# Low parts of query and middle ahead of statistics and norms in VectorE's order, queries split straight from PSUM, and tile addresses at multiples of 512 bytes

## The chip, the cores and the metric

One core of one Trainium2 chip. The time is that of one execution on the device, in microseconds (us), as the median of several runs. The engines are TensorE (PE in the profile, its weight loads PEld), VectorE (DVE), ScalarE (ACT), GpSimd (POOL) and SyncE (SP, which issues most DMAs here).

## What is computed

The input is x, two sequences of 4096 tokens with 512 channels each, so 8192 tokens. The output is the sum of three things: x, an attention branch and a feed-forward branch, both on the normalised x.

```python
xn = layernorm(x)
# attention branch: linear attention, 32 heads of 16 channels
q, k, v = split(relu(xn @ qkv_weight.T))            # each 8192 x 512
vk = einsum('bnhe,bnhd->bhed', [v, 1], k)           # per sequence and head
att = vk_q[..., :16] / (vk_q[..., 16:] + 1e-15)     # vk_q = vk applied to q
y1 = att @ proj_weight.T + proj_bias
# feed-forward branch
cont = sigmoid(xn @ enc_w + enc_b) @ s2c_w + s2c_b  # 512 -> 1024 -> 64
...                                                 # router: the best 2 of 8 experts for each token
moe = sum of w_e * (relu(cont @ e_w1 + e_b1) @ e_w2 + e_b2)   # 64 -> 512 -> 64
rates = sigmoid(moe @ c2s_w + c2s_b)                # 64 -> 1024
y2 = layernorm(sigmoid(rates @ dec_w + dec_b)) * ln_g + ln_b  # 1024 -> 512
out = x + y1 + y2
```

## The kernel before

**Split matmuls.** Every large product is made from float32 values that are split in two: a high part (written as fp32r by ScalarE) and a low part (the value less its high part, by VectorE). `pass3` (L102 to L105) multiplies high weights by the high input, low weights by the high input, and high weights by the low input: three matmuls of 128x128 stationary and 128x512 moving values for each pair of chunks.

**Four stages**, each a block of five engine programs that are written out by hand and tied by semaphores. A block of tokens has 512 tokens (NB = 16), a tile 128 (TT = 64). `front` (A) normalises, transposes and encodes: for each block 8 groups of 12 encoder matmuls (stationary `enc`, moving `xs`), each followed by a pair on `s2c`, with transposes after some. `keyvalue` (B) makes key and value for each tile: 2 x 12 matmuls (L946 to L948; stationary `xs`, moving `wk` or `wv`), then 8 outer products of 258 columns on `kh`, `kl` and `v`. `experts` (C) runs 39 groups of 512 gathered tokens with 4 x 4 matmuls each on `wt`, and two times four transposes between them; SyncE loads each group's expert weights `wt` and tokens `gt`, and stores the result `yo` three groups later; `yo` has three buffers, so VectorE's `close_tile` (L1246) waits for an older store. While this goes on the weights of the last stage are loaded and split. `decode` (D) makes query, attention output, decoder and the sum.

**The decode stage.** TensorE's order for block i, with the second half of block i-1 worked in: for each of four chunks m of the query `query(i, m)` (12 matmuls of `pass3` into the bank bX[m % 2]; stationary `wq`, moving `xsd`); after chunk 0 `middle(i)` (four transposes of the mixture `mo` of both experts' outputs), after chunks 1 and 2 `rates(i, m - 1)` (the content product, L1460 and L1461, on `midh` and `midl`); and `denominators(i, m - 1)` (L1468, L1469, on `qh` and `ql`). Then `attend(i - 1, t)` for four tiles (the output product, L1486 to L1488, 12 matmuls on `qnh`, `qnl` and `mh`, `ml`), four decoder biases, and 8 x 12 decoder matmuls (L1509 to L1511) with six more content products and four `fan` products between them. The banks bX serve the query and the output product in turn, so `attend(i - 1, 0)` waits for the plain query of chunk 2, and `attend(i - 1, 1)` for that of chunk 3.

ScalarE's `query(i, m)` first writes the plain query `q` (relu of the bank, L1370) and then from it the high part `qh` (L1373); then `middle(i)` writes `midh` (L1378), and `rates` takes a tanh (L1384) and its high part (L1392). VectorE's side of the same things is `query` (`ql` from `q` and `qh`, L1572), `middle` (`midl` from the bank and `midh`, L1577) and `rates` (`ratel`, L1582). For block i-1 VectorE also has per tile `stats` (batch statistics of `out`, L1587, and after the fourth the aggregates L1592), `norm` (L1597), `add` (L1605, with the root `rs` that GpSimd makes of the variances, L1334) and `attend` (adds the output product, L1612). GpSimd adds the bias to the next x in four operations (L1354), from the first output addition on. In block 0 there is nothing behind, and TensorE puts `decoder_sum` (16 matmuls, L1494 and L1495) after the query; VectorE works on its result (L1627).

**Addresses.** `Memory.put` places each tile in the first gap that is free in its stages, at a multiple of 32 bytes. The first free byte is 16,512. From the order and the sizes in `place` the starts follow; modulo 512 bytes they are: 224 for `enc`, `xs0`, `xs1`, `s2c` and `wk_h`; 384 for `wk_l`, `wv`, `sph`, `spl`, `kh`, `kl`, `v`, `dec`, `wq`, `c2s`, `fan`, `rc2`, `rows`, `pick_bias`, `mh`, `ml`, `den`, `qh`, `ql`, `qnh`, `qnl`, `rateh` and `ratel`; 0 for `ch`, `cl`, `hidh`, `hidl`, `xsd`, `midh` and `midl`; 128 for `ident`; and 384, 416, 448 and 480 for `wt0` to `wt3`. The chunks inside a tile that matmuls address start at multiples of 512 bytes from the tile's start, except in `v` (rows of 258 values) and in the last part of `wt` (at value 1026).

Of the kernel before, what the change touches and what calls it, by code (L numbers as in the profile page):

```python
# [5 lines left out]
ALU = mybir.AluOpType  # L6
# [6 lines left out]
P = 128  # L13
# [17 lines left out]
DEN_EPS = 1e-15  # L31
VW = 2 * P + 2


NS = 2 * TOK // BLK + NE - 1

E1A, E2, B2, E1B = 0, EH, 2 * EH, 2 * EH + 2
EW = 3 * EH + 2

# [32 lines left out]
class Memory(dict):  # L72


    def __init__(self, nc):
        super().__init__()
        self.nc, self.placed, self.floor = nc, [], (nc.sbuf_base + 31) // 32 * 32

    def put(self, stages, name, shape, dt=F32):
        size = 4  # L80
        for n in shape[1:]:
            size *= n
        size = (size + 31) // 32 * 32
        taken = sorted((a, b) for a, b, s in self.placed if set(s) & set(stages))
        at = self.floor
        for a, b in taken:
            if at + size <= a:
                break
            at = max(at, b)
        assert at + size <= self.nc.sbuf_usable_end, (name, at + size)  # L90
        self.placed.append((at, at + size, stages))
        self[name] = self.nc.alloc_sbuf_tensor_at(name, list(shape), dt, offset=at)
        return at
# [14 lines left out]
def place(nc):  # L108
# [69 lines left out]
    for n in ("kh", "kl"):  # L178
        put("B", n, [P, 2, DIM], F32R)
    put("B", "v", [P, 2, KC, VW], F32R)  # L180
    put("BC", "total", [P, KC, VW])
# [38 lines left out]
    put("Cc", "eo", [P, 2, BLK])  # L220
    put("Cc", "c2s_raw", [P, HID])
    put("Cc", "fanf", [P, KC, P])
    put("Cc", "blank", [P, BLK])
    put("Cc", "pbf", [P, P])
    put("Cc", "onesf", [MOE, BLK])
    put("Cc", "bias2", [P, 2, DIM])
# [610 lines left out]
def keyvalue(nc, d, T, S):  # L837
    with ExitStack() as ctx:
# [95 lines left out]
        def _(pe):  # L934
# [17 lines left out]
            def outer(n):  # L952
# [6 lines left out]
                for g in range(KC):  # L959
                    s = slice(g * P, (g + 1) * P)  # L960
                    pe.matmul(bA[g][:, 0:VW], kh[:, n % 2, s], v[:, n % 2, g, :], start=(n % HALF == 0), stop=False)
                    m = pe.matmul(bA[g][:, 0:VW], kl[:, n % 2, s], v[:, n % 2, g, :], start=False,
                                  stop=(n % HALF == HALF - 1))
# [75 lines left out]
def experts(nc, d, T, S):  # L1039
    with ExitStack() as ctx:  # L1040
# [12 lines left out]
        def _(sp):  # L1053
# [6 lines left out]
            def load_expert(g):  # L1060
                if g >= 4:
# [3 lines left out]
                rows = P if g < 4 else BIAS_ROWS  # L1065
                sp.dma_start(f32(wt[g % 4][:, 0:E1B]), d["ew"][bass.ds(e, 1), :, 0:E1B].rearrange("e p w -> (e p) w"))\
                    .then_inc(S[f"wt_in{g % 4}"], 16)
# [10 lines left out]
            for g in range(NS):  # L1078
# [3 lines left out]
                if g == 2:  # L1082
                    sp.dma_start(T["c2s_raw"][:, :], d["c2s_w"][:, :]).then_inc(S["w_in3"], 16)
                    sp.dma_start(T["dec_raw"][:, :, :], d["dec_w"][:, :].rearrange("p (c n) -> p c n", n=DIM))\
# [5 lines left out]
                if g == 8:  # L1090
                    sp.wait_ge(S["den_out"], BATCH)
                    sp.wait_ge(S["m_done"], BATCH * KC)
                    sp.dma_start(f32(T["xsd"][:, :, :, :]), d["xs"][0]).then_inc(S["xsd_in"], 16)
                if g >= 6:
# [7 lines left out]
        def _(pool):  # L1102
            fanf, pbf = T["fanf"], T["pbf"]
            pool.memset(T["onesf"][:, :], 1.0).then_inc(S["c_consts"], 1)
            pool.wait_ge(S["c_consts"], 1)
# [123 lines left out]
        def _(dve):  # L1229
# [3 lines left out]
            for i in range(2):  # L1233
                dve.tensor_copy(cl[MOE:P, i, :], T["onesf"][:, :]).then_inc(S["cl_ones"], 1)

# [51 lines left out]
def decode(nc, d, T, S, out_dram):  # L1287
    with ExitStack() as ctx:
# [76 lines left out]
        def _(act):  # L1365
            def query(i, m):
                n = i * KC + m
                act.wait_ge(S["q_done"], n + 1)
                wait(act, S["qnl_out"], n - KC + 1)
                act.activation(q[:, m, :], bX[m % 2][:, :], ACT.Relu).then_inc(S["q_out"], 1)  # L1370
                act.wait_ge(S["q_out"], n + 1)
                wait(act, S["den_done"], n - 1)
                act.activation(qh[:, m % 2, :], q[:, m, :], ACT.Copy).then_inc(S["qh_out"], 1)  # L1373

# [25 lines left out]
            for i in range(NB):  # L1400
                for m in range(KC):
                    query(i, m)
                    if m == 0 and i:
                        middle(i)
                    if 1 <= m <= 2 and i:
                        rates(i, m - 1)
                if i == 0:
# [143 lines left out]
        def _(dve):  # L1551
# [16 lines left out]
            def query(i, m):  # L1568
                n = i * KC + m
                dve.wait_ge(S["qh_out"], n + 1)  # L1570
                wait(dve, S["den_done"], n - 1)
                dve.tensor_tensor(ql[:, m % 2, :], q[:, m, :], f32(qh[:, m % 2, :]), ALU.subtract).then_inc(S["ql_out"], 1)  # L1572

# [68 lines left out]
            for i in range(NB + 1):  # L1642
                ahead, behind = i < NB, i > 0
                if behind:
                    for t in range(NT):
                        stats(i - 1, t)
                    norm(i - 1, 0)
                if ahead and behind:
                    query(i, 0)
                    middle(i)  # L1650
                if behind:
                    add(i - 1, 0)
                    norm(i - 1, 1)
                    add(i - 1, 1)
                if ahead and behind:
                    query(i, 1)
                    rates(i, 0)
                if behind:
                    norm(i - 1, 2)
                    norm(i - 1, 3)  # L1660
# [110 lines left out]
```

## Time and profile before

| | us |
|---|---|
| median of 3 runs | 2007.07 (2006.65 to 2007.4) |
| the profiled execution | 2008.04 |
| its span in the trace | 2006.3 |
| stage A, TensorE from and to | 12.7 to 501.5 |
| stage B | 501.5 to 933.2 |
| stage C | 933.2 to 1135.3 |
| stage D | 1135.3 to 2002.7 |

The span is the time between the first and the last instruction that the profile holds; the profiled execution's own time has 1.7 us more around it. Shares of busy time over the span are TensorE 97%, VectorE 53%, ScalarE 41%, GpSimd 19%. The granted clock of TensorE is 0.989 of full over the execution, and full in nearly all slices.

How to read the rows: a row of the timeline is its start, its duration, the engine, the line of the kernel, the operation, output and inputs by name, shapes and number; in brackets stands how long the engine had been idle before it and what ended that. Matmuls are pipelined, so that they overlap in the listing: their pace is the distance of starts.

### The profile page before, as it was taken

What the parts mean: (1) busy time and instruction counts of PE and PEld (TensorE: products, weight loads), DVE (VectorE), ACT (ScalarE), POOL (GpSimd) and SP (SyncE); (2) the same over time, 40 slices, a digit from 0 to 9 for tenths busy, and PEclk for the clock granted to TensorE, in tenths of its full rate; (3) what the DMA queues carried; (4) which work ended last, traced back from release to release, by engine and by line L of the source; (5) the groups of instructions that cost most, each with busy time, mean ns of one, the idle gap of its engine ahead of it and who ended that gap; (6) DMA issues with size and microseconds to landing.
All of it is one profiled execution on the core that took longest, in us unless ns stands there. A gap on an engine that the chain in (4) does not pass through costs nothing. (4 is left out here: it accounts for less than half of the span.)

```text
span 2006.3 us, 24926 instructions
## 1 busy us (share of the span) xinstructions
PE 1944.9 (97%) x8980; PEld 1587.0 (79%) x8980; DVE 1055.2 (53%) x1863; ACT 812.9 (41%) x1359; POOL 390.4 (19%) x428
## 2 busy tenths in 40 slices
PE   7999999998999999998999889999999999999998
PEld 5888888887888888886788668888888888888886
DVE  6555555553442222223888555555555566566654
ACT  4545454544112221113777443443434444344442
POOL 1000000000004444421000212223222222222320
PEclk9999999999999999998999989999999999999999
DMA  5562333342123332223877502222222222221210
GB/s 204 229 226 79 127 150 123 138 153 74 63 88 113 116 113 107 97 82 143 280 231 236 171 24 90 90 90 90 90 89 89 89 88 89 83 69 72 80 69 32
DMA packets 74825, 233.93 MB, mean 117 GB/s; under 512 B 9856, under 2 KB 15952, under 8 KB 68176
## 3 DMA queue, kind: packets, MB, share of 16 engines
q1 hardware_dynamic: 66432, 219.58, 30.7%
q0 software_dynamic: 8272, 12.76, 2.1%
q8 instruction: 72, 1.18, 0.2%
q14 instruction: 49, 0.40, 0.1%
HBM read 151.95 MB, written 80.36 MB: 116 GB/s over the span
## 5 line engine op out<-in xcount | busy, mean ns | idle before, releaser
L103 PE MATMUL A_E<-xs,enc_h 128*128 128x512 f32 x512 | 207.6, 405 | 0.0
L1582 DVE TENSOR_TENSOR ratel<-rate,rateh 128x512 fp32r<-128x512 f32 x128 | 88.4, 691 | 217.4 <-ACT rateh L1392 217.4
L105 PE MATMUL A_E<-xs,enc_h 128*128 128x512 f32 x512 | 202.4, 395 | 0.0
L104 PE MATMUL A_E<-xs,enc_l 128*128 128x512 f32 x512 | 201.7, 394 | 0.0
L1509 PE MATMUL D_D<-dec_h,rateh 128*128 128x512 f32 x512 | 200.0, 391 | 0.0
L1510 PE MATMUL D_D<-dec_l,rateh 128*128 128x512 f32 x512 | 199.9, 390 | 0.0
L1511 PE MATMUL D_D<-dec_h,ratel 128*128 128x512 f32 x512 | 199.4, 389 | 0.0
L1384 ACT ACTIVATE rate<-D_Y,cols 128x512 f32<-128x512 f32 x128 | 87.7, 685 | 264.5 <-PE D_Y L1461 261.6
L571 DVE TENSOR_TENSOR spl<-sp_t,sph 128x512 fp32r<-128x512 f32 x128 | 88.6, 692 | 196.5 <-ACT sph L393 196.5
L871 POOL DMA_INDIRECT slots_scratch<-ctok,idx x128 | 123.5, 964 | 250.6 <-DVE v L999 123.5
L389 ACT ACTIVATE sp_t<-A_E,cols 128x512 f32<-128x512 f32 x128 | 88.1, 688 | 200.3 <-PE A_E L105 198.3
L1341 POOL DMA_INDIRECT ga<-eo_scratch,idx x64 | 66.3, 1036 | 371.6 <-DVE ratel L1582 192.6
L999 DVE SCALAR_TENSOR_TENSOR v<-B_KV,v 128x512 fp32r<-128x512 f32 x64 | 44.3, 692 | 175.0 <-ACT v L900 174.9
L900 ACT ACTIVATE v<-B_KV 128x512 fp32r<-128x512 f32 x64 | 38.4, 600 | 205.2 <-PE B_KV L948 205.2
L1354 POOL TENSOR_TENSOR xd<-xd,bias 128x512 f32<-128x512 f32 x64 | 80.4, 1281 | 178.6 <-DVE out L1612 178.6
L103 PEld LDWEIGHTS A_E<-xs,enc_h 128*128 128x128 f32 x512 | 96.9, 189 | 22.4 <-DVE xs L559 3.2
L105 PEld LDWEIGHTS A_E<-xs,enc_h 128*128 128x128 f32 x512 | 96.5, 189 | 21.9
L104 PEld LDWEIGHTS A_E<-xs,enc_l 128*128 128x128 f32 x512 | 96.9, 189 | 19.6
L1510 PEld LDWEIGHTS D_D<-dec_l,rateh 128*128 128x128 f32 x512 | 96.2, 188 | 20.5
L1511 PEld LDWEIGHTS D_D<-dec_h,ratel 128*128 128x128 f32 x512 | 96.1, 188 | 20.6
L1509 PEld LDWEIGHTS D_D<-dec_h,rateh 128*128 128x128 f32 x512 | 96.2, 188 | 20.5
L993 DVE SCALAR_TENSOR_TENSOR kl<-B_KV,kh 128x512 fp32r<-128x512 f32 x64 | 44.2, 691 | 129.1 <-ACT kh L896 129.1
(283 smaller groups left out, 4748.9 us busy)
## 6 DMA issues: line engine op xcount, KB each, us to landing
xs_scratch<-xs SPq DMA_DIRECT2D x16, 2048.0 KB, 8.5
xsd<-xs_scratch SPq DMA_DIRECT2D x16, 2048.0 KB, 7.9
xs<-xs_scratch SPq DMA_DIRECT2D x14, 2048.0 KB, 8.7
wt<-ew_scratch SPq DMA_DIRECT2D x39, 513.0 KB, 3.8
x<-in_x SPq DMA_DIRECT2D x16, 1024.0 KB, 5.4
xd<-in_x SPq DMA_DIRECT2D x16, 1024.0 KB, 5.2
out_y<-out SPq DMA_DIRECT2D x64, 256.0 KB, 2.0
slots_scratch<-zt SPq DMA_DIRECT2D x1, 9984.0 KB
```

The source lines that it names most:

```text
L103: pe.matmul(out, w_hi, x_hi, start=start, stop=False)
L104: pe.matmul(out, w_lo, x_hi, start=False, stop=False)
L105: return pe.matmul(out, w_hi, x_lo, start=False, stop=stop)
L389: act.activation(T["sp_t"][:, m % 2, :], bE[m % 2][:, :], ACT.Tanh, bias=T["enc_b"][:, m:m + 1], scale=0.5).then_inc(S["sp_out"], 1)
L571: dve.tensor_tensor(T["spl"][:, n % 3, :], T["sp_t"][:, m % 2, :], f32(T["sph"][:, n % 3, :]), ALU.subtract)\
L871: pool.indirect_dma_start(d["slots"][:, :], bass.IndirectOffsetOnAxis(ap=T["idx2" if second else "idx1"][:, t:t + 1], axis=0), T["ctok"][: ...
L1354: pool.tensor_tensor(x[i % 2][:, t, :], x[i % 2][:, t, :], T["bias"][:, :], ALU.add)\
L1384: act.activation(rate[:, k % 2, :], bY[:, :], ACT.Tanh, bias=T["c2s_b"][:, k:k + 1], scale=0.5)\
L1509: pe.matmul(bD[t][:, :], rateh[:, n % 3, o], T["dec_h"][:, k, :], start=False, stop=False)
L1510: pe.matmul(bD[t][:, :], rateh[:, n % 3, o], T["dec_l"][:, k, :], start=False, stop=False)
L1511: m = pe.matmul(bD[t][:, :], ratel[:, n % 3, o], T["dec_h"][:, k, :], start=False, stop=(k == HC - 1))
L1582: dve.tensor_tensor(ratel[:, n % 3, :], rate[:, k % 2, :], f32(rateh[:, n % 3, :]), ALU.subtract)\
```

## The change

1. VectorE's order in `decode`: the low parts of query chunk 0 and of the middle come ahead of the fourth statistic, the aggregates and the first norm; the first two adds come after the low parts of chunk 1 and of the first rates.
2. ScalarE's and VectorE's `query`: the high part is now the relu of the bank itself and is written first, and the low part is taken by VectorE from the bank (the larger of it and 0, less the high part). The plain query is written by ScalarE from the bank after the low part, behind `middle` or `rates`.
3. `Memory.put` starts every tile of 512 bytes or more at a multiple of 512. Rows of `v` are 384 values long (258 used), and the last part of `wt` starts at value 1152. After this every tile that a large matmul reads, and every chunk in it, starts at a multiple of 512 bytes. To make room, `onesf` is dropped (the first rows of `eo` carry the ones), and `c2s_raw` shares memory with a tile of stage B.
4. For that reason the load of `c2s_raw` moves from group 2 of stage C to group 8, ahead of the load of `xsd` and the store of `yo` in SyncE's queue. It is used in group 16.

```diff
-E1A, E2, B2, E1B = 0, EH, 2 * EH, 2 * EH + 2
-EW = 3 * EH + 2
+E1A, E2, B2, E1B = 0, EH, 2 * EH, 2 * EH + P
+EW = 3 * EH + P
...
+        step = 512 if size >= 512 else 32
         size = (size + 31) // 32 * 32
-        at = self.floor
+        at = (self.floor + step - 1) // step * step
         for a, b in taken:
             if at + size <= a:
                 break
-            at = max(at, b)
+            at = max(at, (b + step - 1) // step * step)
...
-    put("B", "v", [P, 2, KC, VW], F32R)
+    put("B", "v", [P, 2, KC, VROW], F32R)
...
                 if g == 2:
-                    sp.dma_start(T["c2s_raw"][:, :], d["c2s_w"][:, :]).then_inc(S["w_in3"], 16)
                     sp.dma_start(T["dec_raw"][:, :, :], d["dec_w"][:, :].rearrange("p (c n) -> p c n", n=DIM))\
...
                 if g == 8:
                     sp.wait_ge(S["den_out"], BATCH)
                     sp.wait_ge(S["m_done"], BATCH * KC)
+                    sp.dma_start(T["c2s_raw"][:, :], d["c2s_w"][:, :]).then_inc(S["w_in3"], 16)
                     sp.dma_start(f32(T["xsd"][:, :, :, :]), d["xs"][0]).then_inc(S["xsd_in"], 16)
...
             def query(i, m):
                 n = i * KC + m
                 act.wait_ge(S["q_done"], n + 1)
+                wait(act, S["den_done"], n - 1)
+                act.activation(qh[:, m % 2, :], bX[m % 2][:, :], ACT.Relu).then_inc(S["qh_out"], 1)
+                if m == 0 and i:
+                    middle(i)
+                if 1 <= m <= 2 and i:
+                    rates(i, m - 1)
+                act.wait_ge(S["ql_out"], n + 1)
                 wait(act, S["qnl_out"], n - KC + 1)
                 act.activation(q[:, m, :], bX[m % 2][:, :], ACT.Relu).then_inc(S["q_out"], 1)
-                act.wait_ge(S["q_out"], n + 1)
-                wait(act, S["den_done"], n - 1)
-                act.activation(qh[:, m % 2, :], q[:, m, :], ACT.Copy).then_inc(S["qh_out"], 1)
...
                 dve.wait_ge(S["qh_out"], n + 1)
                 wait(dve, S["den_done"], n - 1)
-                dve.tensor_tensor(ql[:, m % 2, :], q[:, m, :], f32(qh[:, m % 2, :]), ALU.subtract).then_inc(S["ql_out"], 1)
+                dve.scalar_tensor_tensor(out=ql[:, m % 2, :], in0=bX[m % 2][:, :], scalar=0.0,
+                                         in1=f32(qh[:, m % 2, :]), op0=ALU.max, op1=ALU.subtract)\
+                    .then_inc(S["ql_out"], 1)
...
                 if behind:
-                    for t in range(NT):
+                    for t in range(NT - 1):
                         stats(i - 1, t)
-                    norm(i - 1, 0)
                 if ahead and behind:
                     query(i, 0)
                     middle(i)
                 if behind:
-                    add(i - 1, 0)
+                    stats(i - 1, NT - 1)
+                    norm(i - 1, 0)
                     norm(i - 1, 1)
-                    add(i - 1, 1)
                 if ahead and behind:
                     query(i, 1)
                     rates(i, 0)
                 if behind:
+                    add(i - 1, 0)
+                    add(i - 1, 1)
                     norm(i - 1, 2)
                     norm(i - 1, 3)
```

## Rows read from the trace of the kernel before

**Rows 1.** The page: busy time of each engine, share of the span, instructions.

```profile
PE 1944.9 (97%) x8980; PEld 1587.0 (79%) x8980; DVE 1055.2 (53%) x1863; ACT 812.9 (41%) x1359; POOL 390.4 (19%) x428
```

**Rows 2.** Waits of PE: who waited for whom, us, times, longest.

```profile
PE D_Y L1460 <- DVE midl L1577: 9.7, 16, 1.4
```

**Rows 3.** Timeline of all engines, one decode block.

```profile
1513.09 2.47 DVE L1587 BATCH_NORM_STATS2 st<-out 128x6 f32<-128x512 f32 x4
...
1514.30 0.60 ACT L1370 ACTIVATE q<-D_X 128x512 f32<-128x512 f32 x1 [1.60 <-PE D_X L105]
...
1515.46 0.58 ACT L1378 ACTIVATE midh<-D_Y 128x512 fp32r<-128x512 f32 x1
...
1516.01 0.79 DVE L1597 SCALAR_TENSOR_TENSOR out<-out,mv,ln_g 128x512 f32<-128x512 f32 x1
...
1517.10 0.40 PE L105 MATMUL D_X<-xsd,wq_h 128*128 128x512 f32 x1
...
1518.06 0.50 PE L1460 MATMUL D_Y<-midh,c2s 128*128 128x512 f32 x1 [0.56 <-DVE midl L1577]
...
1518.39 0.39 PE L1461 MATMUL D_Y<-midl,c2s 128*128 128x512 f32 x1
```

**Rows 4.** Timeline of PE: starts in runs of stage A, B and D.

```profile
203.62 0.40 PE L104 MATMUL A_E<-xs,enc_l 128*128 128x512 f32 x1
...
205.48 0.39 PE L103 MATMUL A_E<-xs,enc_h 128*128 128x512 f32 x1
...
206.16 0.40 PE L476 MATMUL A_S<-sph,s2c 128*128 128x512 f32 x1
...
600.07 0.40 PE L946 MATMUL B_KV<-wv_h,xs 128*128 128x512 f32 x1
...
605.41 0.40 PE L948 MATMUL B_KV<-wk_h,xs 128*128 128x512 f32 x1
...
1511.31 0.40 PE L103 MATMUL D_X<-xsd,wq_h 128*128 128x512 f32 x1
...
1513.87 0.39 PE L105 MATMUL D_X<-xsd,wq_h 128*128 128x512 f32 x1
...
1529.22 0.39 PE L1486 MATMUL D_X<-mh,qnh 128*128 128x512 f32 x1
...
1537.16 0.39 PE L1488 MATMUL D_X<-mh,qnl 128*128 128x512 f32 x1
```

**Rows 5.** Timeline of the end: the first add of the last block.

```profile
1990.28 0.75 DVE L1605 SCALAR_TENSOR_TENSOR out<-out,rs,xd 128x512 f32<-128x512 f32 x1 [0.96 <-POOL rs L1334]
```

**Rows 6.** Timeline of decode block 0.

```profile
1145.75 4.99 POOL L1354 TENSOR_TENSOR xd<-xd,bias 128x512 f32<-128x512 f32 x4
...
1147.30 4.61 DVE L1572 TENSOR_TENSOR ql<-q,qh 128x512 fp32r<-128x512 f32 x2 [2.57 <-ACT qh L1373]
...
1148.82 0.40 PE L105 MATMUL D_X<-xsd,wq_h 128*128 128x512 f32 x1
...
1151.36 0.50 PE L1468 MATMUL D_Y<-qh,den 128*128 128x512 f32 x1 [2.14 <-DVE ql L1572]
...
1153.07 0.63 PE L1494 MATMUL D_D<-dec_h,ones 128*128 128x512 f32 x1
...
1156.94 0.39 PE L1495 MATMUL D_D<-dec_l,ones 128*128 128x512 f32 x1
```

**Rows 7.** Timeline of a steady decode block: GpSimd's bias additions.

```profile
1529.74 5.03 POOL L1354 TENSOR_TENSOR xd<-xd,bias 128x512 f32<-128x512 f32 x4 [12.04 <-DVE out L1612]
...
1532.14 0.69 DVE L1612 TENSOR_TENSOR out<-D_X,out 128x512 f32<-128x512 f32 x1 [1.42 <-PE D_X L1488]
```

**Rows 8.** Timeline of stage C and list of DMA issues (KB, us to landing).

```profile
973.75 0.37 SPq L1093 DMA_DIRECT2D xsd<-xs_scratch  x1
...
984.10 0.69 DVE L1246 TENSOR_REDUCE yo<-C_Y 128x256 f32<-128x512 f32 x1 [3.42 <-DMA eo_scratch<-yo]
...
c2s_raw<-in_c2s_w SPq DMA_DIRECT2D x1, 512.0 KB, 3.6
```

More of the change, by code:

```diff
@@ L32 @@
 VW = 2 * P + 2
+VROW = 3 * P
 NS = 2 * TOK // BLK + NE - 1
-E1A, E2, B2, E1B = 0, EH, 2 * EH, 2 * EH + 2
-EW = 3 * EH + 2
+E1A, E2, B2, E1B = 0, EH, 2 * EH, 2 * EH + P
+EW = 3 * EH + P
 BIAS_ROWS = 80
@@ L220, in place @@
     put("Cc", "eo", [P, 2, BLK])
-    put("Cc", "c2s_raw", [P, HID])
+    put("c", "c2s_raw", [P, HID])
     put("Cc", "fanf", [P, KC, P])
@@ L224, in place @@
     put("Cc", "pbf", [P, P])
-    put("Cc", "onesf", [MOE, BLK])
     put("Cc", "bias2", [P, 2, DIM])
@@ L960, in outer @@
                     s = slice(g * P, (g + 1) * P)
-                    pe.matmul(bA[g][:, 0:VW], kh[:, n % 2, s], v[:, n % 2, g, :], start=(n % HALF == 0), stop=False)
-                    m = pe.matmul(bA[g][:, 0:VW], kl[:, n % 2, s], v[:, n % 2, g, :], start=False,
+                    pe.matmul(bA[g][:, 0:VW], kh[:, n % 2, s], v[:, n % 2, g, 0:VW], start=(n % HALF == 0), stop=False)
+                    m = pe.matmul(bA[g][:, 0:VW], kl[:, n % 2, s], v[:, n % 2, g, 0:VW], start=False,
                                   stop=(n % HALF == HALF - 1))
@@ L1065, in load_expert @@
                 rows = P if g < 4 else BIAS_ROWS
-                sp.dma_start(f32(wt[g % 4][:, 0:E1B]), d["ew"][bass.ds(e, 1), :, 0:E1B].rearrange("e p w -> (e p) w"))\
+                sp.dma_start(f32(wt[g % 4][:, 0:B2 + 2]), d["ew"][bass.ds(e, 1), :, 0:B2 + 2].rearrange("e p w -> (e p) w"))\
                     .then_inc(S[f"wt_in{g % 4}"], 16)
@@ L1103, in _ @@
             fanf, pbf = T["fanf"], T["pbf"]
-            pool.memset(T["onesf"][:, :], 1.0).then_inc(S["c_consts"], 1)
+            pool.memset(T["eo"][0:MOE, 0, :], 1.0).then_inc(S["c_consts"], 1)
             pool.wait_ge(S["c_consts"], 1)
@@ L1233, in _ @@
             for i in range(2):
-                dve.tensor_copy(cl[MOE:P, i, :], T["onesf"][:, :]).then_inc(S["cl_ones"], 1)
+                dve.tensor_copy(cl[MOE:P, i, :], T["eo"][0:MOE, 0, :]).then_inc(S["cl_ones"], 1)
             def content(g):
@@ L1402, in _ @@
                     query(i, m)
[L1403 to L1406, printed above, removed]
                 if i == 0:
```

## Prediction

> **What bounds the kernel now.** I read the page first: it says which engine is full. TensorE is busy for 97% of the span [rows 1], so time can go in two ways only: TensorE waits less, or its own instructions follow each other more closely. The list of waits comes next. Its largest entry inside the steady loop is the content product's wait for `midl`, 16 times [rows 2]. To see what that costs, the timeline of one decode block is read in order [rows 3]; to see how closely matmuls follow each other, I take the starts of long runs without a wait and divide by the intervals [rows 4]. The listed durations (0.39 or 0.40 us) overlap and don't show it; the starts do.
>
> Order in the block [rows 3]: the last matmul of the second query chunk starts at 1517.10, the next could start 0.23 later, at 1517.33. It starts at 1518.06, and its successor only 0.33 after it. So 0.73 + 0.10 = 0.83 us are lost. What is late is `midl`. Its inputs are there early: `midh` starts at 1515.46 (0.58 long). VectorE meanwhile does four statistics, the aggregates and a norm up to 1516.80, and only then `ql` and `midl`.
>
> **Part 1: VectorE's and ScalarE's order.** In the new order three statistics (4 take 2.47, so 3 take 1.86) end at 1514.95. ScalarE writes `qh` as its first action on the product, so from 1514.30 for about 0.60, to 1514.90; `midh` follows to 1515.5. VectorE: `ql` 1514.95 to 1515.65, `midl` to 1516.35. TensorE wants it at 1517.33: one us to spare. The stall goes: 15 blocks x 0.83 = 12.4 us (the sixteenth wait is block 0's, where all is serial).
>
> Who is late next? I drop the 1500 of the times. Behind `midl` (16.35) come the fourth statistic and the aggregates (about 1.1 together, by the pace of the same rows), two norms (1.5) and `ql` of chunk 1, written by about 19.7; its high part is ready at 18.1. TensorE wants it after the content product, the first denominators, twelve query matmuls and the next content product: 17.33 + 18 x 0.23 = 21.5. Then come the low rates, two adds and two norms (3.7) and `ql` 2, by 24.0, wanted at 24.7. ScalarE now holds the plain query back until `ql` is written, and behind it in its queue stand the next chunk's high part and rates. Plain chunk 2 is there at 24.7, and TensorE's output product needs its bank at 25.2; plain chunk 3 at 27.5, wanted at 28.4. The tanh of the rates stands ahead of the new wait and isn't delayed. POOL's root is ready 0.96 after a norm of 0.79 [rows 3, 5], 1.75 behind the aggregates, so at 19.2; the adds now stand at 20.3. The thinnest place has 0.5 us. I take no new stall; with that cover gone, each 0.1 us of lateness costs 15 x 0.1 = 1.5 us. The bounds of this part are 0 and 12.4.
>
> In the last block a norm now fills the wait of 0.96 us for POOL's root [rows 5]: 0.7 us, on the chain that ends the kernel.
>
> **Part 2: the low part straight from PSUM.** One instruction for one instruction, both 128x512. In steady blocks nothing changes. In block 0 it does [rows 6]: POOL adds the bias from 1145.75 to 1150.74, and two `ql` instructions of VectorE take 4.61, where others of this size take 0.69 each [rows 7]. TensorE's denominators start at 1151.36 where they could have started at 1149.05, and the decoder's sum behind them runs partly with durations of 0.63 in place of 0.39 (the granted clock's 1.2 GHz level). The last of its 16 matmuls starts at 1156.94; without stall and at full clock it is 1149.05 + 17 x 0.227 = 1152.91. Difference 4.0 us. VectorE's first work after it waits for that sum, so all of it is passed on. Would the new instruction be held up as well? It reads one tile in PSUM and one in SBUF, as the output addition does, and that one takes 0.69 in the middle of POOL's four additions [rows 7]. So 4.0 us; bounds 0 and 4.0.
> The Trainium skill (SBUF — State Buffer, section "SBUF: two separate sides") states a lock between VectorE with two SBUF inputs and a GpSimd operation that reads SBUF; the trace agrees (4.61 against 0.69), and the sum is the same by it.
>
> **Part 3: addresses.** Offsets are those of the section on the kernel, in bytes modulo 512. Four kinds of run without waits [rows 4]:
> - output product, stationary 384, moving 384: (1537.16 - 1529.22) / 35 = 226.9 ns
> - query, stationary 384, moving 0: (1513.87 - 1511.31) / 11 = 232.7 ns
> - key and value, stationary 224, moving 224 or 384: (605.41 - 600.07) / 23 = 232.2 ns
> - encoder, 224 and 224, behind transposes: the first 8 intervals 232.5 ns, the next 3 (206.16 - 205.48) / 3 = 226.7 ns.
>
> The encoder and the query run the same three lines in the same pattern, and only one of them settles at 227. So neither the pattern nor a multiple of 64 bytes decides (224 isn't one). What fits all four is whether the two operands have the same offset: then the pace settles at 227 after some 8 matmuls, otherwise it stays near 232.5. After the change all matmul operands are at 0. The sum:
> - query: 768 matmuls x 5.8 ns = 4.5 us
> - key and value: 1536 x 5.3 = 8.1, less 64 settlings after the outer products, each 8 x 5.6 = 45 ns, 2.9: 5.2 us
> - encoder: half of 128 groups of twelve follow only the `s2c` pair (224 on 384), which I take as what unsettles them: 64 x 45 ns = 2.9, and the pairs themselves, 256 x 3 ns = 0.8: 3.7 us
> - experts: 624 matmuls, but transposes come every 4 or 12: at most 3.6, I take 1
> - decoder: 96 content pairs (384 on 0) between fast matmuls, about 0.02 us each (half a settling): 1.9 us
>
> Together 16 us. It could be nothing (0), or up to 22 if nothing has to settle any more.
> The opposing rule in the Trainium skill is on the same page and in the same section: within the engine side only the port pair that VectorE and GpSimd share causes contention, and TensorE waits on nobody. By it addresses do nothing for matmuls, and that is the first rival. The two paces of one code [rows 4] speak against it.
>
> **Part 4: the moved load.** `c2s_raw`, 512 KB, now stands in SP's queue before the 2048 KB of `xsd` and the store of `yo` behind that. In the trace that store is what VectorE waits for at 984.10, 3.42 us, and TensorE behind VectorE [rows 8]. `xsd` and the store behind it take from 973.75 to 984.0, so some 4.9 us for each MB: 512 KB more is 2.5 us, all of it on the path, at the slow 1.2 GHz level perhaps a little more. Bounds: 0 (if the transfers overlap better) and 3.6, its own time to landing [rows 8]. I take 2.5. At its old place its absence lets the weights behind it land earlier, at nothing to 0.5. Memory set from another tile, the 1536-byte row of `v`, 512 bytes of padding in `wt`: the same instructions and bytes, nothing.
>
> **Sum.** 12.4 + 0.7 + 4.0 + 16 - 2.5 = 30.6. The profiled execution took 2008.04; 2008.04 - 30.6 = 1977.4. The median is 1.0 lower than the profiled execution: 1976.
>
> **Rivals.**
> 1. Addresses do nothing. For it: no row varies the address alone. Against: the same code at two paces. 2007.1 - 14.6 = 1992.
> 2. The plain query is held too long. ScalarE's queue waits for `ql`, and the output product or the denominators stall in place of the content product. For it: ScalarE's new wait, with 0.5 us of slack at its thinnest. Against: that slack. It gives the 12.4 us back: 1988. The point is a `ql` of chunk 2 more than 0.5 us later than worked out.
> 3. Offset 0 is itself the slow one, not the difference. For it: `xsd`, `ch`, `cl` and `midh` are all moving operands at 0, and all their runs are slow. Against: key and value are slow without a 0. Then nothing gains and the fast runs join the slow: some 150 matmuls a block x 16 plus half of the encoder's 1536, 3170 x 5.8 ns = 18.4 us. 2007.1 - 14.6 + 18.4 = 2011, slower. It decides from a pace of about 231.5 ns in the output product on.
> 4. More than forecast: everything settles, and the outer products (258 columns) tighten as well: 1966.
>
> **Numbers.** Forecast 0.62, rival 1 0.20, rival 2 0.07, rival 3 0.07, rival 4 0.04. The forecast's own range is 1968 to 1984: parts 3 and 4 between half and full. The range for 8 in 10 must reach rival 1, the largest other case: 1967 to 1994. A difference of 0.2% (4 us) is about what can be told from no change. Faster 0.92 (all but rival 3 and a bad mix), within 0.2% 0.04, slower 0.04.
>
> **What would show it.** Order: the wait for `midl` is left in block 0 only, and the content product starts 0.23 after the query; a block is shorter by 0.83 + (4.5 + 1.9) / 16 = 1.2 us. PSUM: no `ql` over 0.75 us, none of TensorE's waits on `ql`, and the sum in block 0 without matmuls of 0.63. Addresses: starts in the query 227 apart and in key and value after some 8 matmuls. Load: the wait for the `yo` store near 6 us. Wrong it would be if query starts stay 232.7 apart, or a wait of the output product or the denominators shows up 15 times.

## The result and the profile after

| | before | after |
|---|---|---|
| median, us (4 runs each) | 2007.24 (2006.65 to 2007.52) | 1971.43 (1969.36 to 1973.64) |
| the profiled execution | 2008.04 | 1971.89 |
| its span | 2006.3 | 1970.1 |
| stage A, TensorE from its start to its end | 488.8 | 483.2 (12.5 to 495.7) |
| stage B | 431.7 | 421.8 (to 917.5) |
| stage C | 202.1 | 203.5 (to 1121.0) |
| stage D | 867.4 | 845.5 (to 1966.5) |

The ratio is 0.9822 [0.9805, 0.9839] (in brackets the 95% interval, here and below): the kernel is faster by 35.8 us. Forecast were 1976 (31 us) and a range of 1967 to 1994. The table says at once where to look: 21.9 us come from the decode stage, 9.9 and 5.6 from B and A, in which nothing but addresses was changed, and stage C lost 1.4.

The page, busy time of each engine. TensorE is as full as before [rows 1], and its busy time is 26.4 us less for the same number of instructions:

```profile
PE 1918.5 (97%) x8980; PEld 1586.5 (81%) x8980; DVE 1049.0 (53%) x1863; ACT 809.9 (41%) x1359; POOL 390.8 (20%) x428
```

The waits of PE (us in total, times, longest), from the second of the list on:

```profile
PE C_O L1212 <- DVE hidl L1261: 6.1, 4, 3.6
PE D_X L1488 <- DVE out L1616: 3.9, 1, 3.9
PE D_Y L1453 <- DVE mo L1565: 3.8, 1, 3.8
...
PE D_Y L1462 <- DVE midl L1581: 1.4, 1, 1.4
```

The wait for `midl`, 9.7 us in 16 times [rows 2], is left once, in block 0. Nothing has taken its place: no wait of the output product, the denominators or the content product that comes 15 times. The first line is the largest wait of the experts' products; it was 5.2 us before.

Timeline of one decode block, VectorE, ScalarE and TensorE in order:

```profile
1488.93 1.87 DVE L1591 BATCH_NORM_STATS2 st<-out 128x6 f32<-128x512 f32 x3
...
1490.07 0.60 ACT L1372 ACTIVATE qh<-D_X 128x512 fp32r<-128x512 f32 x1 [1.54 <-PE D_X L108]
1490.56 0.59 ACT L1384 ACTIVATE midh<-D_Y 128x512 fp32r<-128x512 f32 x1
1490.71 0.67 DVE L1574 SCALAR_TENSOR_TENSOR ql<-D_X,qh 128x512 fp32r<-128x512 f32 x1
1491.31 0.68 DVE L1581 TENSOR_TENSOR midl<-D_Y,midh 128x512 fp32r<-128x512 f32 x1
...
1492.85 0.39 PE L108 MATMUL D_X<-xsd,wq_h 128*128 128x512 f32 x1
1493.08 0.39 PE L1462 MATMUL D_Y<-midh,c2s 128*128 128x512 f32 x1
...
1498.41 0.68 DVE L1574 SCALAR_TENSOR_TENSOR ql<-D_X,qh 128x512 fp32r<-128x512 f32 x1
...
1499.12 0.60 ACT L1379 ACTIVATE q<-D_X 128x512 f32<-128x512 f32 x1 [0.38 <-DVE ql L1574]
...
1500.78 0.39 PE L1488 MATMUL D_X<-mh,qnh 128*128 128x512 f32 x1
```

Read against [rows 3]: `midl` ends at 1491.99, and the content product starts at 1493.08, 0.23 behind the last matmul of the query. It had 1.09 us to spare (forecast: one us). The thinnest place of the new order is the plain query of chunk 2: ScalarE ends it at 1499.72, the output product needs its bank at 1500.78, so 1.06 us are left where 0.5 was forecast.

Timeline of block 0:

```profile
1131.39 5.04 POOL L1356 TENSOR_TENSOR xd<-xd,bias 128x512 f32<-128x512 f32 x4
...
1133.50 0.69 DVE L1574 SCALAR_TENSOR_TENSOR ql<-D_X,qh 128x512 fp32r<-128x512 f32 x1 [2.79 <-ACT qh L1372]
...
1135.30 0.39 PE L108 MATMUL D_X<-xsd,wq_h 128*128 128x512 f32 x1
...
1139.45 0.40 PE L1497 MATMUL D_D<-dec_l,ones 128*128 128x512 f32 x1
```

In the middle of GpSimd's additions `ql` takes 0.69, where two took 4.61 [rows 6]. From the query's last matmul to the decoder sum's last it is 4.15 us, and it was 1156.94 - 1148.82 = 8.12.

Timeline of PE: starts in runs of stage A (behind transposes, and behind the pair on `s2c`), B (right behind the outer products, and the next half) and D:

```profile
201.19 0.39 PE L107 MATMUL A_E<-xs,enc_l 128*128 128x512 f32 x1
...
203.48 0.39 PE L108 MATMUL A_E<-xs,enc_h 128*128 128x512 f32 x1
...
204.16 0.39 PE L106 MATMUL A_E<-xs,enc_h 128*128 128x512 f32 x1
...
205.97 0.39 PE L108 MATMUL A_E<-xs,enc_h 128*128 128x512 f32 x1
...
584.64 0.40 PE L948 MATMUL B_KV<-wv_h,xs 128*128 128x512 f32 x1
...
587.16 0.39 PE L950 MATMUL B_KV<-wv_h,xs 128*128 128x512 f32 x1
587.39 0.39 PE L948 MATMUL B_KV<-wk_h,xs 128*128 128x512 f32 x1
...
589.88 0.39 PE L950 MATMUL B_KV<-wk_h,xs 128*128 128x512 f32 x1
...
1493.98 0.39 PE L106 MATMUL D_X<-xsd,wq_h 128*128 128x512 f32 x1
...
1496.48 0.39 PE L108 MATMUL D_X<-xsd,wq_h 128*128 128x512 f32 x1
```

The query goes at (1496.48 - 1493.98) / 11 = 227.3 ns, where it went at 232.7 [rows 4]. Key and value: (587.16 - 584.64) / 11 = 229.1 ns behind the outer products, then (589.88 - 587.39) / 11 = 226.4. The encoder: (203.48 - 201.19) / 10 = 229.0 behind transposes, and (205.97 - 204.16) / 8 = 226.3 right behind the pair on `s2c`, which no longer unsettles anything.

A run of matmuls settles, as I call it, when its starts come to stand some 226.6 ns apart. To add this up I took every distance from the start of a 512-column matmul to the start of the next matmul, if it is under 260 ns, in each stage, less 226.6 ns each, and call the sum the excess:

| excess over 226.6 ns a matmul, us | A | B | C | D | sum |
|---|---|---|---|---|---|
| before | 7.8 | 9.8 | 3.1 | 8.2 | 28.9 |
| after | 2.5 | 1.8 | 2.2 | 1.65 | 8.2 |
| gain | 5.3 | 8.0 | 0.9 | 6.6 | 20.7 |

With only those distances counted in which the next matmul has 512 columns too, the gain is 20.2 us.

Timeline of stage C, the queue of SyncE and what follows:

```profile
958.28 0.37 SPq L1094 DMA_DIRECT2D c2s_raw<-in_c2s_w  x1
958.69 0.43 SPq L1095 DMA_DIRECT2D xsd<-xs_scratch  x1
959.17 0.43 SPq L1076 DMA_DIRECT2D eo_scratch<-yo  x1
...
969.45 0.69 DVE L1248 TENSOR_REDUCE yo<-C_Y 128x256 f32<-128x512 f32 x1 [4.27 <-DMA eo_scratch<-yo]
...
970.79 0.80 PE L1212 MATMUL C_O<-hidh,wt 128*128 128x512 f32 x1 [3.61 <-DVE hidl L1261]
971.38 0.63 PE L1213 MATMUL C_O<-hidl,wt 128*128 128x512 f32 x1
```

VectorE's wait for the store is 4.27 us, 0.85 more than before [rows 8]. Behind it TensorE waits 3.61 us (before 2.73), and then 11 of its 512-column matmuls run at the 1.2 GHz level (durations of 0.63; the granted clock is 0.50 of full from 973.3 to 976.4); before there were 5. Such a matmul starts some 0.43 us behind its predecessor in place of 0.23, so six more are 1.2 us.

### The profile page after: what moved, and what is told of

It is laid out like the page before. It is cut to its first block and busy times, and to the rows that moved or that the text cites. A ratio compares the mean times of both kernels' runs of the same rounds, so it can differ in the third digit from the quotient of the medians.

```text
span 1970.1 us, 24926 instructions
## 1 busy us (share of the span) xinstructions
PE 1918.5 (97%) x8980; PEld 1586.5 (81%) x8980; DVE 1049.0 (53%) x1863; ACT 809.9 (41%) x1359; POOL 390.8 (20%) x428
## 5 line engine op out<-in xcount | busy, mean ns | idle before, releaser
L1512 PEld LDWEIGHTS D_D<-dec_l,rateh 128*128 128x128 f32 x512 | 96.4, 188 | 20.2
```

The source lines that it names most:

```text
L1512: pe.matmul(bD[t][:, :], rateh[:, n % 3, o], T["dec_l"][:, k, :], start=False, stop=False)
```

## The experiments

Each kernel is compared with the kernel before on the same chip; the medians of before there are 2005.93 (e1, e2, e3, e5), 2005.63 (e4, e6, e7) and 2006.36 (e8, e9). "Before" and "after" in the edits are the two kernels of this study.

**e1: the addresses alone.** Everything of the change but the decode stage's code, which is that of before.

Two of the lines of after that it takes back:

```diff
-                for t in range(NT - 1):
+                for t in range(NT):
                     stats(i - 1, t)
...
-                act.activation(qh[:, m % 2, :], bX[m % 2][:, :], ACT.Relu)
+                act.activation(q[:, m, :], bX[m % 2][:, :], ACT.Relu)
```

> The kernel after with the decode stage's code of before: addresses, the row of v, the padding of wt and the moved load stay; the new order and the low part from PSUM are undone. Theory of the prediction, with the sizes that the trace after shows (stage A 5.6 us shorter, B 9.9 shorter, C 1.4 longer, and in D matmuls after matmuls some 6.6 us closer): 2007.2 - 20.7 = 1986.5. The wait for midl (15 x 0.56 to 0.74) and the long ql of block 0 are back. Rival (the addresses do little and the order gave most of the 36 us): 1995 or more, with query starts still near 232 apart.

Measured: 1988.17 (1986.07 to 1990.25), ratio 0.9913 [0.9897, 0.993], 17.8 us less than before. The excess is 2.6, 1.8, 2.2 and 2.1 us in A to D, as after. The waits of PE:

```profile
PE D_Y L1462 <- DVE midl L1579: 11.3, 16, 1.4
PE C_O L1212 <- DVE hidl L1261: 6.3, 5, 3.6
...
PE D_Y L1470 <- DVE ql L1574: 2.4, 1, 2.4
```

What follows: half of the gain is made by tile addresses, with no matmul of the loops that got faster added, dropped or reordered. (The moved load, which costs time, is in e1 as well.) The first line holds something that I had not worked out: the wait for `midl` is 11.3 us, 1.6 more than before, since a query that ends earlier only leads to a longer wait. Addresses alone therefore lose 1.6 us that the new order gives back.

**e2: order and PSUM alone.** The kernel before with the decode code of after.

Two of the places (memory, `v`, `wt` and the load of `c2s_raw` are those of before):

```diff
-                act.activation(q[:, m, :], bX[m % 2][:, :], ACT.Relu)
+                act.activation(qh[:, m % 2, :], bX[m % 2][:, :], ACT.Relu)
...
-                for t in range(NT):
+                for t in range(NT - 1):
                     stats(i - 1, t)
```

> The kernel before with the decode stage's code of after: new order and low part from PSUM, addresses and loads as before. Theory: 12.4 + 4.0 + 0.7 us, 2007.2 - 17.1 = 1990; starts of key, value and query stay at 232 to 233 apart, the wait for midl is gone in 15 blocks. Rival (addresses alone): 2003 or more. If the two parts add up, e1 and e2 together give 1986.5 + 1990 - 2007.2 = 1969.3, against 1971.4 measured for the whole.

Measured: 1988.65 (1988.14 to 1989.15), ratio 0.9913 [0.9897, 0.993], 17.3 us less. The excess is that of before (7.7, 9.8, 3.2 and 7.95 us), and the wait for `midl` is left in block 0 alone (1.4 us, once). The two halves together, 0.87% and 0.87%, make 1.74%; the whole change made 1.78%. They add up within the error.

**e5: VectorE's order alone.** As e2, but `ql` is still taken from the plain query in SBUF, and the plain query is still written first.

```diff
-                    for t in range(NT):
+                    for t in range(NT - 1):
                         stats(i - 1, t)
-                    norm(i - 1, 0)
                 if ahead and behind:
                     query(i, 0)
                     middle(i)
                 if behind:
-                    add(i - 1, 0)
+                    stats(i - 1, NT - 1)
+                    norm(i - 1, 0)
                     norm(i - 1, 1)
-                    add(i - 1, 1)
                 if ahead and behind:
                     query(i, 1)
                     rates(i, 0)
                 if behind:
+                    add(i - 1, 0)
+                    add(i - 1, 1)
```

> The kernel before with VectorE's new order alone: ScalarE writes the plain query first and VectorE takes ql from two SBUF tiles, as before. Theory: qh is 0.6 us later than in the whole change, midl still ends at about 1517.0 of the old clock against 1517.33 wanted, so the stall of 0.83 goes in 15 blocks and 0.7 us at the end: 2007.2 - 13.1 = 1994. Block 0 keeps its ql of 4 us and TensorE's wait of 2.1 behind it. So e5 less e2 is the price of the PSUM part: 4.0 us. Rival (the split from PSUM is what makes room for midl): the wait for midl stays, smaller, and the time is 1999 or more.

Measured: 1991.04 (1990.86 to 1991.26), ratio 0.9926 [0.9909, 0.9942], 14.9 us less. So point 2 of the change (the low part from PSUM, together with ScalarE's new order) is worth 1991.04 - 1988.65 = 2.4 us, not 4.0. It lies in block 0 (the table below: 6.59 - 4.17 = 2.42): from the first to the last of the 16 `midl` both kernels take as long, 762.5 and 762.4 us. In the steady blocks VectorE's order alone removes the stall. One line's view in e5 and in e2 (duration in ns, least, median, most), each in its own fence:

```profile
L1572 DVE TENSOR_TENSOR ql<-q,qh x64: 676/692/4035, 1140.3 to 1932.6; 128x512 fp32r<-128x512 f32 x64
```

```profile
L1572 DVE SCALAR_TENSOR_TENSOR ql<-D_X,qh x64: 676/691/693, 1138.5 to 1929.3; 128x512 fp32r<-128x512 f32 x64
```

One of 64 takes 4.0 us when both inputs are in SBUF, and none does when one is in PSUM; the median is the same. The two lines agree with the lock that the Trainium skill describes (SBUF — State Buffer, "SBUF: two separate sides"), between VectorE with two SBUF inputs and a GpSimd operation that reads SBUF: 4.035 against 0.693 us at most. The operation changed with the source, so that the lines alone don't separate the two.

Why 2.4 and not 4.0 can be read from the same stretch as above, the query's last matmul to the decoder sum's last, in every kernel:

| | ql from | us |
|---|---|---|
| before | SBUF | 8.12 |
| e5 | SBUF | 6.59 |
| e1 | SBUF | 6.80 |
| e9 (below) | SBUF | 6.81 |
| e2 | PSUM | 4.17 |
| after | PSUM | 4.15 |

With the stall at full clock it is 2.4 to 2.7 us more than without. Only in the profiled execution of before did 8 matmuls behind it run at the 1.2 GHz level (the granted clock is 0.69 of full from 1151.4 to 1156.9), another 1.3 to 1.5 us; e1, e5 and e9 have the same stall (2.2 to 2.4 us) and none there. Whether most executions of before have these 8, the one profile of it can't say.

**e3: all at 224 instead of 0.** After, with every tile of 512 bytes or more at 224 modulo 512.

```diff
+PHASE = 224
...
-        at = (self.floor + step - 1) // step * step
+        def up(b):
+            return (b - PHASE + step - 1) // step * step + PHASE
+        at = up(self.floor)
```

> The kernel after with every tile of 512 bytes or more at 224 modulo 512 in place of 0: no operand is at a multiple of 64 bytes, all differences are 0. Theory (the difference between the two operands decides): the same as after, 1971, starts 227 apart in key, value and query. Rival (multiples of 512, or of 64, decide by themselves): starts near 232, 7300 matmuls x 5.5 ns = 40 us at most, 1990 to 2011.

Measured: 1972.21 (1971.27 to 1972.8), ratio 0.9832 [0.9815, 0.9848]. Key and value, the half behind the values' half, timeline of PE:

```profile
588.93 0.39 PE L953 MATMUL B_KV<-wk_h,xs 128*128 128x512 f32 x1
...
591.42 0.39 PE L955 MATMUL B_KV<-wk_h,xs 128*128 128x512 f32 x1
```

(591.42 - 588.93) / 11 = 226.4 ns, as after. No large tile is at a multiple of 512, or even of 64, and all is as fast. What decides is how the two operands stand to each other. Rival 3, offset 0 as the slow one, was refuted by the result itself, where every operand is at 0 and the runs are fast.

**e4: single differences.** After, with some tiles moved so that a product's operands differ: `xsd` by 256, `qnh` and `qnl` by 128, `rateh` and `ratel` by 64, `xs` by 32.

```diff
+PHASE = {'xsd': 256, 'qnh': 128, 'qnl': 128, 'rateh': 64, 'ratel': 64, 'xs0': 32, 'xs1': 32}
...
+        phase = PHASE.get(name, 0) if step == 512 else 0
```

> The kernel after with tiles of one product moved against each other, a different distance in each stage: xsd at 256 modulo 512 (wq at 0), qnh and qnl at 128 (mh and ml at 0), rateh and ratel at 64 (dec at 0), xs0 and xs1 at 32 (enc, wk and wv at 0). It asks how fine the rule is. If any difference modulo 512 unsettles a run, all four settle nowhere: the output product and the decoder go to 232 (2300 matmuls x 5.5 ns = 13 us), the query to 232.7 (4.5), encoder, key and value back to their old pace (15): about 2003. If only a difference in the low bits counts (a multiple of 64 is as good as 0), then the query, the output product and the decoder stay at 227 and stage A and B alone are slow: 1986. The rival that no rule of addresses holds (the pace came from something else in the change): 1971.

Measured: 2004.45 (2002.02 to 2005.94), ratio 0.9996 [0.9986, 1.0007]. The whole gain is gone, though the new order is in: the decoder, the encoder and the output product, which were fast or half fast before, are now slow as well. All but one product behave as expected. Timeline of PE, a query chunk and then two tiles of the output product:

```profile
1514.32 0.39 PE L111 MATMUL D_X<-xsd,wq_h 128*128 128x512 f32 x1
...
1516.81 0.39 PE L113 MATMUL D_X<-xsd,wq_h 128*128 128x512 f32 x1
...
1524.38 0.40 PE L1493 MATMUL D_X<-mh,qnh 128*128 128x512 f32 x1
...
1529.75 0.39 PE L1495 MATMUL D_X<-mh,qnl 128*128 128x512 f32 x1
```

The output product (128 apart) goes at (1529.75 - 1524.38) / 23 = 233.5 ns. The query, 256 apart, goes at (1516.81 - 1514.32) / 11 = 226.4: as fast as with no difference at all. "The same offset modulo 512" was too narrow.

**e8: is the period 256?** After, with 256 between the operands of the encoder, of key and value and of the decoder, and 128 in the query (`xsd` 128) and in the output product (`qnh`, `qnl` 384).

```diff
+PHASE = {'xs0': 256, 'xs1': 256, 'rateh': 256, 'ratel': 256, 'qnh': 384, 'qnl': 384, 'xsd': 128}
```

> The kernel after with other distances between the two operands: xs0 and xs1 at 256 modulo 512 (encoder, key and value), rateh and ratel at 256 (decoder), qnh and qnl at 384 (output product), xsd at 128 (query); enc, wk, wv, dec, mh, ml and wq stay at 0. e4_differences found 256 as good as 0 in the query and 128, 64 and 32 bad. Theory (what counts is the difference modulo 256): encoder, key, value and decoder stay at 227, the output product (384, which is 128 modulo 256) goes to 232 to 233 and the query (128) too: 768 x 6 ns each = 9 us, 1980. Rival (256 was good in the query for a reason of the query's own): the decoder's 1536 and stage A and B slow as well, 2003.

Measured: 1980.61 (1979.87 to 1982.31), ratio 0.9871 [0.9856, 0.9887]. Key and value, and the output product:

```profile
595.45 0.39 PE L953 MATMUL B_KV<-wk_h,xs 128*128 128x512 f32 x1
...
597.94 0.39 PE L955 MATMUL B_KV<-wk_h,xs 128*128 128x512 f32 x1
...
1506.89 0.39 PE L1493 MATMUL D_X<-mh,qnh 128*128 128x512 f32 x1
...
1515.03 0.40 PE L1495 MATMUL D_X<-mh,qnl 128*128 128x512 f32 x1
```

226.4 ns with 256 between the operands, (1515.03 - 1506.89) / 35 = 232.6 with 384. The rule passed a test that was made for it. All kernels together, mean distance of starts (those under 260 ns) over all matmuls of a product:

| difference of starts modulo 256 | product and kernel | ns |
|---|---|---|
| 0 | output product, before / after | 227.2 / 226.7 |
| 0 | query, after / e3 | 227.5 / 227.5 |
| 0 (256) | query e4; decoder e8 | 228.2; 227.1 |
| 0 (256) | key halves of key and value, e8 | 226.7 |
| 32 | key and value, e4; encoder, e4 | 233.2; 232.7 |
| 64 | decoder, e4 | 233.2 |
| 128 | query, before / e8 | 232.6 / 232.5 |
| 128 | output product, e4 / e8 | 233.2 / 232.6 |
| 160 | value, before | 233.9 |
| 0 for `wk_h`, 160 for `wk_l` | key, before | 232.1 |

The last row says that the rule holds for a run as a whole: two of three key matmuls had equal offsets before, and with every third at 160 the run didn't settle.

**e9: the smallest edit.** The kernel before, with `xsd` at 384 modulo 512, where `wq` is.

```diff
             at = max(at, b)
+        if name == "xsd":
+            at = (at - 384 + 511) // 512 * 512 + 384
```

> The kernel before with one tile moved: xsd starts at 384 modulo 512 in place of 0, like wq (the tiles behind it move on by 384 bytes); all code and all other offsets of matmul operands as before. Theory: the query's 768 matmuls settle at 227: 4.5 us less than before, 0.2%, and all other paces unchanged. Rival (a single tile says nothing, the pace hangs on the whole layout or on the order): no change in the query's starts.

Measured: 2001.4 (1998.78 to 2002.93), ratio 0.9976 [0.9966, 0.9987], 5.0 us less. Timeline of PE, one query chunk:

```profile
1504.39 0.39 PE L106 MATMUL D_X<-xsd,wq_h 128*128 128x512 f32 x1
...
1506.88 0.39 PE L108 MATMUL D_X<-xsd,wq_h 128*128 128x512 f32 x1
```

226.4 ns. The excess of D falls from 8.2 to 2.15, and in A, B and C it stays (8.0, 9.9, 3.2). The 6.1 us in D are more than the query's: the first free gap behind the moved `xsd` puts `midh` and `midl` at 384 too, where `c2s` is, so that the content pairs settle as well. And they are more than the 5.0 measured, for the reason of e1: the wait for `midl` grows from 9.7 to 11.3. 6.1 - 1.6 = 4.5.

**e6: the moved load, three groups earlier.** After, with `c2s_raw` loaded at group 5 instead of 8.

```diff
+                if g == 5:
+                    sp.wait_ge(S["den_out"], BATCH)
+                    sp.wait_ge(S["m_done"], BATCH * KC)
+                    sp.dma_start(T["c2s_raw"][:, :], d["c2s_w"][:, :]).then_inc(S["w_in3"], 16)
                 if g == 8:
-                    sp.dma_start(T["c2s_raw"][:, :], d["c2s_w"][:, :]).then_inc(S["w_in3"], 16)
```

> The kernel after with the load of c2s_raw at group 5 of stage C in place of group 8 (with the same two waits for the memory, moved with it), so that no other large load stands ahead of xsd and the store. Theory: VectorE's wait for the yo store falls from about 4.3 to about 3.4 or less, and TensorE's matmuls at the low clock behind it from 11 to 6: 1 to 2.5 us less than after, 1969 to 1970.5. Rival (the extra wait in the trace after has another cause): the wait stays as long, 1971.4.

Measured: 1970.41 (1968.0 to 1971.03), ratio 0.9819 [0.9803, 0.9836]. In the trace the wait for the store of `yo` is 3.6 us (before 3.4, after 4.3), TensorE's for `hidl` 5.6 in all, and 6 matmuls behind it are slow instead of 11; in time the difference from after can't be told from none. So the cost of the moved load is read from the traces alone.

**e7: `xsd` in parts.** As e6, and `xsd` is loaded in eight parts of 256 KB, one every third group, each behind a store of `yo`.

```diff
                 if g == 8:
-                    sp.dma_start(f32(T["xsd"][:, :, :, :]), d["xs"][0]).then_inc(S["xsd_in"], 16)
...
                     store(g - 6)
+                if g >= 9 and g % 3 == 0 and g < 33:
+                    h, c = divmod((g - 9) // 3, KC)
+                    sp.dma_start(f32(T["xsd"][:, h, c, :]), d["xs"][0][:, h, c, :]).then_inc(S["xsd_in"], 16)
...
-                    pe.wait_ge(S["xsd_in"], 16 * i + 16)
+                    pe.wait_ge(S["xsd_in"], 16 * i + 16 * 2 * KC)
```

> The kernel of e6_c2s_early with the 2048 KB of xsd loaded in 8 parts of 256 KB, one behind the store of every third group from group 9 on. Theory: no store waits behind a long transfer, VectorE's wait for the yo store and the low clock behind it are gone: 3.8 + 2.2 us less than after, 1965.5. Rival (the queues are nearly full in this stage, and the delay only spreads): several waits for stores or weights of 1 us each, and 1969 or more.

Measured: 1966.35 (1965.02 to 1967.78), ratio 0.9801 [0.9785, 0.9817]: 4.1 us under e6, with no overlap of the two kernels' runs, and the fastest kernel of this study. The groups by line, and the waits of PE:

```profile
L1250 DVE TENSOR_REDUCE yo<-C_Y 128x256 f32<-128x512 f32 x39 | 26.3, 674 | 1.7 <-PE C_Y L1188 1.7
```

```profile
PE C_O L1214 <- DVE hidl L1263: 2.7, 4, 1.1
```

VectorE waits for no store at all; the slowest of the 39 landed 5.6 us after its issue, where it was 10.0 in e6. TensorE's wait for `hidl` is 2.7 us where e6 has 5.6, and the stretch of slow matmuls in the middle of stage C isn't there: 2.9 + 6 x 0.2 = 4.1 us. Stage C takes 197.4 us, 3.7 less than in e6 and 6.1 less than after. The cost that the moved load added to was there before the change, and it goes when the 2 MB transfer no longer stands ahead of a store in one piece. e7 changed both the size of the parts and their place in the queue; which of the two does it isn't shown.

## Why the prediction held, and where its sizes were off

Against the profiled executions the sum was 30.6 us, and 2008.04 - 1971.89 = 36.15 came. The terms, with what the traces give for each:

| term | forecast | by the traces |
|---|---|---|
| order in steady blocks | 12.4 | 12.4 |
| last block | 0.7 | 0.8 |
| `ql` from PSUM, block 0 | 4.0 | 4.0 in these two executions, 2.4 by e5 and e2 |
| addresses | 16 | 20.7 |
| moved load | -2.5 | -0.9, and -1.2 for slow matmuls behind it |
| extents of the 1.2 GHz level elsewhere | 0 | +0.6 |

They sum to 36.4 (the outer products' 0.5, below, isn't among them). The last row counts the 512-column matmuls at the low level that the rows above it don't hold, 61 before and 58 after, at 0.2 us each.

**Order: right, in mechanism and size.** Forecast was a block shorter by 1.2 us. The 16 `midl` stand from 1162.9 to 1938.9 before and from 1145.4 to 1902.9 after: (776.0 - 757.5) / 15 = 1.23 us; without the first distance, which holds the end of block 0, the median block went from 52.72 to 51.45, so 1.27. The stall itself can be read in e5, which has before's addresses: from the last query matmul of chunk 1 to the second content matmul it is 1.289 us in mean before and 0.466 in e5, and 15 x 0.823 = 12.3. Rival 2, the plain query held too long, didn't happen: the wait that it needs is in no list, and the thinnest place has 1.06 us. e5 measured order and last block at 14.9, 1.7 more than the 13.2 of the two rows. If most executions of before have the 8 matmuls at the low level that e5 has not, they explain 1.3 to 1.5 of it; but the runs of before also range over 4.5 us, so that this stays open. In the last block TensorE's wait for `out` fell from 4.7 to 3.9.

**PSUM: right, but priced with something that isn't the stall's alone.** The step is "without stall and at full clock it is 1149.05 + 17 x 0.227 = 1152.91. Difference 4.0 us". The stall itself was 2.14 [rows 6]; most of the rest were matmuls at the low level, which three other executions with the same stall had not. The term is 2.4 by e5 and e2, which differ in point 2 of the change alone, and 4.0 only against an execution that has them.

**Addresses: right rule, too small a term, and too narrow a rule.** The step that failed in size is "Together 16 us"; 20.7 came, inside its bounds of 0 to 22. Rival 1 (nothing) is refuted by e1, e4 and e9, rival 3 by the result and by e3. The part on each product:
- key and value: 5.2 forecast, 8.0 by the excess. I took the slow pace from one run, 232.2 ns, where the mean over the stage is 233.0 and the excess with it 9.8 in place of 8.1. And a settling was taken as 45 ns; behind the outer products the first 11 distances are 229.1 in place of 226.6, so 11 x 2.5 = 27 ns, 64 times 1.8 us instead of 2.9.
- encoder: 3.7 forecast, 5.3. As supposed, the `s2c` pair unsettles nothing now; groups behind transposes still settle, but at 10 x 2.4 = 24 ns, the whole stage at 2.5 us.
- query and decoder: 6.4 forecast, 6.6.
- experts: 1 forecast, 0.9. The 4 or 12 matmuls between transposes are too few to settle, as supposed.

In direction this is rival 4: nearly everything settles. Its other half, tighter outer products, is small: 120.6 to 119.4 ns, 448 times, 0.5 us.
That addresses matter for a matmul at all is not what the Trainium skill leads one to expect (SBUF — State Buffer, "SBUF: two separate sides": TensorE never waits on anyone at its port). e1 with 17.8 us and e4 with the whole gain lost say that it is so here. The pace changes with all engines' instructions as they were (e9), so that nothing here contradicts the rule on contention between engines; it only doesn't cover this.

**Moved load: right place, too dear.** The step "512 KB more is 2.5 us, all of it on the path" took the rate of one large transfer for the increment. From `xsd`'s issue to the yo store's landing it was 984.10 - 973.75 = 10.35 us; from `c2s_raw`'s issue it is now 969.45 - 958.28 = 11.17 us: 0.82 more for 512 KB more, a third of what that rate says. Why so little isn't shown. The wait for the store, forecast near 6 us, came out at 4.27. The remark that at the slow level it might cost a little more was worth more than a remark: 1.2 us of 2.1. But these slow matmuls vary (e1 has the same wait of 3.6 us and 5 of them, after has 11), and e6 couldn't show the difference in time. That the term came out near its forecast, -2.1 against -2.5, is luck: two sizes were off in opposite directions.

What stays open: why an address difference that is not a multiple of 256 bytes keeps consecutive matmuls from settling at 226.6 ns. The runs show the rule, for 128x128 stationary and 128x512 moving operands of four bytes, and nothing of its cause. Other shapes and differences other than those in the table weren't looked at one by one.

## What to carry to other kernels

Where TensorE is full, measure the distance between the starts of its matmuls, not their listed durations: one code at two paces is a finding, and here it held 20.7 us where the largest stall of the steady loop held 12.4. Before pricing a stall by one execution, look at whether the matmuls behind it ran at the low clock, and whether they do so behind the same stall in another kernel's trace. And when a faster stage stands ahead of a wait, part of its gain goes into the wait until that is removed too: 1.6 of 20.7 us here.

## What was unexpected of the hardware

- Stationary and moving operands whose start addresses in SBUF differ by 0 or 256 bytes modulo 512 let runs of 512-column matmuls settle at 226.6 ns; with 32, 64, 128 or 160 modulo 256 they stay at 232 to 234. The absolute address is of no account (e3: 1972.21, after: 1971.43).
- A pair with other operands, but the same difference, between two runs doesn't unsettle them (226.3 ns right behind `s2c`); four transposes or eight outer products cost some 25 ns.
- How many 512-column matmuls ran at the 1.2 GHz level behind nearly the same wait differed between executions: in stage C 5 (e1) and 11 (after) behind 3.6 us and none (e4) behind 3.4; in block 0 8 (before) and none (e1, e5, e9) behind 2.1 to 2.4 us.
- The slowest store of 128 KB on the queue that held a load of 2 MB landed 9.8 us (before) and 10.2 us (after) after its issue, 4 us being the median of all 39; with the load cut in eight parts, each behind a store, none took over 5.6.
